# Loads of k and q in quarters, v's rows stored earlier, weight pieces spread over six heads

## The reference

```
h = ln(x) * (1 + scale_msa) + shift_msa
q, k, v = h @ Wq + bq, h @ Wk + bk, h @ Wv + bv      # split into 16 heads of 32
A = softmax(q k^T / sqrt(32));  out = A v
x = x + gate_msa * (out @ Wo + bo)
h2 = ln(x) * (1 + scale_mlp) + shift_mlp
y = x + gate_mlp * (gelu(h2 @ W1 + b1) @ W2 + b2)
```

## Time and profile before

| | us |
|---|---|
| median of 3 runs | 2544.93 (2541.89 to 2549.74) |
| the profiled execution | 2552.45 |
| its span | 2550.7 |
| TensorE busy | 2414.3 (95%) |
| VectorE busy | 1745.4 (68%) |
| ScalarE busy | 1423.4 (56%) |
| GpSimd busy | 1502.3 (59%) |
| DMA, mean over the span | 82 GB/s |

### The profile page before, as it was taken

How to read it: one execution, slowest core, us unless ns; L and a number is a source line. 1 busy time by engine, 2 the same in 40 slices (tenths; PEclk the granted TensorE clock), 3 DMA queues, 4 the chain that set the end, 5 groups by cost and what they waited for, 6 DMA issues and landing times.

```text
span 2550.7 us, 49502 instructions
## 1 busy us (share of the span) xinstructions
PE 2414.3 (95%) x19544; PEld 1358.2 (53%) x19544; DVE 1745.4 (68%) x2878; ACT 1423.4 (56%) x2622; POOL 1502.3 (59%) x706
## 2 busy tenths in 40 slices
PE   6999855899999999999999999999999888999998
PEld 4788642344444444444444444444444346888887
DVE  4444544788888888887888888788878326666563
ACT  3233203577777777777777777777777542222221
POOL 0000103488788878887887888788878634232330
PEclk9999986799999999999999999999999888999999
DMA  7655532122222222222222222222222111332200
GB/s 268 208 171 186 137 110 89 45 75 58 67 72 71 58 68 72 66 62 69 75 57 66 75 69 57 67 77 62 61 71 74 49 50 39 93 103 68 66 34 34
DMA packets 204948, 210.33 MB, mean 82 GB/s; under 512 B 112384, under 2 KB 145152, under 8 KB 195328
## 3 DMA queue, kind: packets, MB, share of 16 engines
q1 hardware_dynamic: 202224, 205.56, 26.9%
q10 hardware_dynamic: 2512, 1.86, 0.3%
HBM read 146.30 MB, written 60.82 MB: 81 GB/s over the span
## 4 chain that ended last, share of the span: by engine, by line
PE 83%; DMA 8%; DVE 3%; ACT 3%; issue 2%; SPq 1%; POOL 0%; ACTq 0%; POOLq 0%; DVEq 0%
PE ps L1216 19%; PE ps L1347 19%; PE ps L1313 9%; PE ps L1325 9%; PE ps L1456 7%; PE ps L1338 7%; PE ps L1327 5%; PE ps L1329 4%; DMA partial_sums<-work 4%; PE ps L1334 2%; DMA q_lo<-work 2%; DVE part_max L1042 1%; ACT work L813 1%; PE ps L1225 1%; DMA tmp<-in_wo 1%
## 5 line engine op out<-in xcount | busy, mean ns | idle before, releaser
L686 POOL TENSOR_TENSOR work<-work 128x1024 f32<-128x1024 f32 x576 | 1351.5, 2405 | 413.9 <-PE ps L1338 223.1
L1042 DVE TENSOR_REDUCE part_max<-ps 128x1 f32<-128x512 f32 x1984 | 1233.2, 682 | 287.7 <-PE ps L1313 287.5
L835 ACT ACTIVATE work<-ps 128x512 f32<-128x512 f32 x2048 | 1058.4, 603 | 355.2 <-PE ps L1334 323.3
L1347 PE MATMUL ps<-work 128*32 128x512 f32 x4096 | 557.7, 617 | 0.2 <-ACT work L835 0.2
L1313 PE MATMUL ps<-acts_r 32*128 32x512 f32 x1344 | 419.2, 480 | 24.7 <-DVE part_max L1042 18.7
L1216 PE MATMUL ps<-acts_r,weights_r 128*128 128x512 f32 x1536 | 383.6, 400 | 4.9 <-DVE acts_r L962 3.8
L1216 PEld LDWEIGHTS ps<-acts_r,weights_r 128*128 128x128 f32 x1536 | 293.5, 193 | 70.2 <-issue 6.8
L1325 PE MATMUL ps<-acts_r 32*128 32x512 f32 x1408 | 300.9, 475 | 28.9 <-DVE work L975 20.0
L1325 PEld LDWEIGHTS ps<-acts_r 32*128 32x128 f32 x1408 | 145.8, 187 | 339.4 <-DVE part_max L1042 176.6
L1327 PE MATMUL ps<-acts_r 32*128 32x512 f32 x1408 | 260.9, 401 | 0.0
L1313 PEld LDWEIGHTS ps<-acts_r 32*128 32x128 f32 x1344 | 181.5, 186 | 140.5 <-DVE part_max L1042 111.4
(11 more groups left out here) (88 smaller groups left out, 2542.9 us busy)
## 6 DMA issues: line engine op xcount, KB each, us to landing
acts_r<-k_hi SPq DMA_DIRECT2D x32, 1024.0 KB
acts_r<-k_lo SPq DMA_DIRECT2D x32, 1024.0 KB
work<-in_x SPq DMA_DIRECT2D x16, 1024.0 KB, 5.4
q_hi<-work SPq DMA_DIRECT2D x32, 256.0 KB, 2.6
q_lo<-work SPq DMA_DIRECT2D x32, 256.0 KB, 3.3
k_hi<-work SPq DMA_DIRECT2D x32, 256.0 KB, 2.6
k_lo<-work SPq DMA_DIRECT2D x32, 256.0 KB, 3.2
v_rows<-work SPq DMA_DIRECT2D x32, 256.0 KB, 2.0
```

What stands on the lines that cost most here:

```text
L686: nc.gpsimd.tensor_tensor(psum_acc[:, at], first, prob[:, t % RING, at], ALU.add).then_inc(add_ok, 1)
L835: nc.scalar.activation(prob[:, t % RING, j * CH:(j + 1) * CH], ps[:, bank, :], ACT.Exp, scale=SCALE).then_inc(exp_ok, 1)
L1042: nc.vector.tensor_reduce(part_max[:, r * TT + q // NQ, q % NQ:q % NQ + 1], ps[:, bank, :], AX.X, ALU.max).then_inc(a_max, 1)
L1347: mm = nc.tensor.matmul(ps[j * DH:(j + 1) * DH, O_BANK, :], v_sb[g % TWO][:, t, :], prob[:, t % RING, j * CH:(j + 1) * CH], start=(t == 0) ...
```

## The change

`load_k` and `load_q` issue four transfers of 32 rows each, one for each row group, instead of one transfer whose outermost dimension is 4; the counts that are waited for (`LOADS_HI`, `LOADS_LO`) follow. In SP's list chunk 7's first four stores come between k_hi and k_lo of head 0, and v's tiles 1 to 3 before head 1's loads. The first two late pieces are loaded before the loads of v of head 1, q_lo and k_lo of head 1 and q_hi and k_hi of head 2; the others two by two at the end of SP's turns for heads 0 to 4. ACT and VectorE split them at steps 4 and 11 of heads 0 to 5. Head 0 makes no maxima in step 0, and has four extra sets, at steps 3, 6, 9 and 12, instead of three.

```diff
-EXTRA_AT = (2, 6, 10)
+EXTRA_AT = (3, 6, 9, 12)
-LOADS_HI, LOADS_LO, LOADS_0 = 2, 3, 6
+LOADS_HI, LOADS_LO, LOADS_0 = 2 * NQ, 2 * NQ + 1, 6
...
-                if g < G - 2 or g == G - 2 and t < NT - LEAD:
+                if (g or t) and g < G - 2 or g == G - 2 and t < NT - LEAD:
...
-        LATE_STEP = 2
+        LATE_STEPS = (4, 11)
+        LATE_HEADS = len(late) // len(LATE_STEPS)
...
             def load_k(dst, src, g, done):
-                rows = src[1][g * DH:(g + 1) * DH, :].rearrange("(o d) q -> o d q", o=1).broadcast_to((NQ, DH, L))
-                sp.dma_start(dst.bitcast(F32), rows).then_inc(done, 16)
+                for r in range(NQ):
+                    sp.dma_start(dst[r * DH:(r + 1) * DH, :].bitcast(F32), src[1][g * DH:(g + 1) * DH, :]).then_inc(done, 16)
 
             def load_q(dst, src, g, done):
-                rows = src[0][g * DH:(g + 1) * DH, :].rearrange("d (r q) -> r d q", q=CH)
-                sp.dma_start(dst.bitcast(F32), rows).then_inc(done, 16)
+                for r in range(NQ):
+                    sp.dma_start(dst[r * DH:(r + 1) * DH, :].bitcast(F32),
+                                 src[0][g * DH:(g + 1) * DH, r * CH:(r + 1) * CH]).then_inc(done, 16)
...
+            def load_late(g):
+
+                for k in range(g * len(LATE_STEPS), (g + 1) * len(LATE_STEPS)):
+                    if k >= 2:
+                        sp.wait_ge(late_hi, k - 1)
+                        sp.wait_ge(late_lo, k - 1)
+                    sp.dma_start(tmp3[:, k % 2, :], late[k][0]).then_inc(late_in[k % 2], 16)
+
             def head(g):
...
                 store_head(g - 1, (g - 1) % TWO)
+                if g + 1 < LATE_HEADS:
+                    load_late(g + 1)
...
             load_k(k_hi[0], qk_hi, 0, hi_in[0])
+            store_qk(NCHUNK - 1, *ORDER[NCHUNK - 1], range(KC))
             load_k(k_lo[0], qk_lo, 0, lo_in[0])
-            store_qk(NCHUNK - 1, *ORDER[NCHUNK - 1])
+            store_qk(NCHUNK - 1, *ORDER[NCHUNK - 1], range(KC, 2 * KC))
             store_v(NCHUNK - 1, *ORDER[NCHUNK - 1], range(1))
             sp.wait_ge(a_max, FILLS)
             load_q(q_hi[0], qk_hi, 0, hi_in[0])
+            store_v(NCHUNK - 1, *ORDER[NCHUNK - 1], range(1, 3))
             put_max(0, 0)
+            store_v(NCHUNK - 1, *ORDER[NCHUNK - 1], range(3, TT))
             load_hi(1, 1)
-            store_v(NCHUNK - 1, *ORDER[NCHUNK - 1], range(1, TT))
-            for k, (rows, _) in enumerate(late):
-                if k == 0:
-                    sp.wait_ge(ada_mm, ADA)
-                if k >= 2:
-                    sp.wait_ge(late_hi, k - 1)
-                    sp.wait_ge(late_lo, k - 1)
-                sp.dma_start(tmp3[:, k % 2, :], rows).then_inc(late_in[k % 2], 16)
-                if k == 1:
-                    sp.wait_ge(qkv_mm, NCHUNK * MM_CHUNK)
-                    stored(NCHUNK)
-                    load_v(1, 1)
-                    load_hi(2, 2)
-                    load_lo(1, 1)
+            sp.wait_ge(ada_mm, ADA)
+            load_late(0)
+            sp.wait_ge(qkv_mm, NCHUNK * MM_CHUNK)
+            load_v(1, 1)
+            load_lo(1, 1)
+            load_hi(2, 2)
+            stored(NCHUNK)
             put_max(1, 1)
+            load_late(1)
...
-            probs(0, {LATE_STEP + k: lambda k=k: split_late_hi(k) for k in range(len(late))})
+            probs(0, late_pieces(0))
...
-            head(0, {LATE_STEP + k: lambda k=k: split_late_lo(k) for k in range(len(late))})
-            for g in range(1, G - 1):
-                head(g)
+            for g in range(G - 1):
+                first = g * len(LATE_STEPS)
+                head(g, {t: lambda k=first + i: split_late_lo(k) for i, t in enumerate(LATE_STEPS) if g < LATE_HEADS})
```

More of the change, by code:

```diff
@@ L840, in probs, with late_pieces @@
                         between[t]()
-            probs(0, {LATE_STEP + k: lambda k=k: split_late_hi(k) for k in range(len(late))})
+            def late_pieces(g):
+                first = g * len(LATE_STEPS)
+                return {t: lambda k=first + i: split_late_hi(k) for i, t in enumerate(LATE_STEPS) if g < LATE_HEADS}
+            probs(0, late_pieces(0))
             for i in range(2):
@@ L845, in _ @@
             for g in range(1, G - 1):
-                probs(g)
+                probs(g, late_pieces(g))
             def split_first_oT(half):
```

## The result

| | before | after |
|---|---|---|
| median of 5 runs, us | 2544.93 (2540.25 to 2549.74) | 2524.05 (2520.45 to 2527.38) |
| the profiled execution | 2552.45 | 2520.45 |
| its span | 2550.7 | 2518.7 |

The change makes the kernel faster by 0.8%: ratio 0.9921, 95% interval 0.9903 to 0.994, which is 20.9 us between the medians. The forecast was 80.6 us, and 2524 us lies outside its range.

A forecast was written before the change was run, and what follows sets the result against it. TensorE was taken to bound the kernel, busy 95% of the span, with stops around head 0's start. Terms -19.7 - 18.8 - 38.1 - 4.0 = -80.6 us took 2544.9 to 2464 us, range 2440 to 2494.

The forecast's parts named there:

- Rival (a): Loads of q and k: quarter transfers no faster than whole ones, rate near 100 GB/s; +25, 2489 us; chance 0.10.
- Parts 1 and 2: Before head 0: chunk 7's stores between split k loads, -19.7 us; v's rows ahead of head 1's loads, -18.8 us.
- The fifth product's margin of 0.3 us: Chunk 7: the fifth product's store lands at about 335 us, wanted by ACT at 335.3.
- Rival (e): Chunk 7 and v's rows: half of the stops stays, 20 us each not won; 2504 us; chance 0.07.
- (b): Head 0: the new waits don't come, clock stays up, extra maxima cost 0.8 us each; 2447 us; chance 0.20.
- Part 3: Head 0: two weight pieces instead of twelve, with new waits and extra maxima; 60.2 against 98.3 us, -38.1 us.
- Part 4: Heads after head 0: faster loads -6 us, ten weight pieces in heads 1 to 5 +2 us; -4 us in all.
- Rival (c): Heads 1 to 5: weight pieces break VectorE's rhythm and the banks, 2.5 us each; +23, 2487 us; chance 0.10.
- The other heads: Heads after head 0: 50.12 us on average against 49.74 at best, 11 us to win; faster loads taken as -6.
- Rival (d): Every head: loads on all engines delay the store of partial sums, stopping ACT and TensorE; 2578 us; chance 0.03.

The follow-up runs named there:

- e5: The kernel before with only the q and k loads in four transfers of 32 rows each; 2503.0 us, ratio 0.9825.
- e6: The kernel of e4 with the q and k loads whole again, as before; 2512.7 us.
- e4: The changed kernel with the weight pieces moved to steps 15, 0 and 1, where GpSimd is idle; 2471.7 us, ratio 0.9706.
- e1: The changed kernel with VectorE's half of each weight piece a maximum with one SBUF input, remainders left out; 2491.6 us.
- e2: The changed kernel with VectorE's half of each weight piece done for one column of 512, both inputs in SBUF; 2516.3 us.
- e3: The changed kernel with VectorE's half of each piece one step after ACT's, at steps 5 and 12; 2510.3 us.
- e8: The changed kernel with GpSimd instead of VectorE making the remainders of the weight pieces, between its additions; 2467.9 us, ratio 0.9689.

## Why the prediction was wrong, point by point

**Four engines against sixteen, right.** From 325 to 330 us after, with k_lo in flight:

```profile
325.00:330.00 5.00, 5.00 (x24) 4.03 (x23) 4.52 (x8) 0.96 (x2) 0.00 (x0) 1.00 1.03 204
```

Share 1.03 at 204 GB/s, where I had taken 200 to 215. e5 and e6 show the cause by doing and undoing that part alone. Rival (a) is out, and with it, for loads of this shape, the rule of the Trainium skill, page DMA: Bandwidth & Descriptors, section Rules for kernel authors, against two transfers to disjoint halves of the partitions instead of one over all 128: the traces don't agree with it for a transfer that stood at a share of 0.25.

**Parts 1 and 2, right.** -38.5 us forecast up to the first score, -40.1 measured after the 2.6 us that came from elsewhere. The fifth product's margin of 0.3 us did not hold: ACT sat idle 4.43 us for its store, 3.04 of them its usual pace, so it was 1.4 us late. TensorE stands nowhere over 0.8 us in these stretches. Rival (e), that half of the stops stays, did not come about; its 2504 counted both stops whole, and half of 18.3 and 20.0 us would have been 19 us, 2483. Nor did (b): head 1's loads did stop TensorE, for 7.3 us.

**Part 3, right in kind, too large by 15.6 us.** Head 1's loads cost 7.3 us, not 4, inside the bound of 8; the waits for the first maxima and exponentials, forecast at 1 and 1.6, were 0.2 and none, so that these three come to 7.5 where 6.6 was forecast. The two pieces were taken as free in head 0 and cost two stops of 2.1 and 2.4 us with a low clock after each. e4 has no piece in head 0's steps 4 and 11 and takes 419.25 - 350.50 = 68.8 us instead of 75.7: so 7 us of the miss are the pieces. Of the other 8 to 9, 1 is the waits; the rest is the clock behind them (0.50 still from 360 to 365 us) and the extra maxima, and how these share it was not taken apart.

**Part 4, the step that failed.** The prediction counted each of the ten pieces in heads 1 to 5 as 0.69 us of VectorE and 0 to 0.8 us of TensorE, "I take 0.2: +2"; they cost 46 to 49 us (+46.3 against before, 297.2 - 5 x 49.74 = 48.5 against a head that runs full), nearly 5 us each. The 48.5 are 31.7 us in which TensorE stands and 17.1 in which it works longer for the same matmuls (265.1 us busy in the five heads against 5 x 49.59 in a head that runs full), at a clock of 0.93 instead of 1.00. Three things were mis-sized in a row:

- The duration. I took 0.69 us from one row. The group of that line over head 0 of before was in the trace, in the view of groups by line (count, busy us, mean ns):

```profile
L1074 DVE TENSOR_TENSOR weights_r<-tmp,weights_r 128x512 fp32r<-128x512 f32 x12 | 14.9, 1242 | 29.6 <-ACT weights_r L795 29.6
```

 A mean of 1242 ns where the least is 691 says that something else holds the operation, and in before's head 0 GpSimd was busy for only 43.0 of 98.3 us, so even this mean was too low for a full head, where it is 2.5 us in the median. e1, e2 and e4 show that it is the second SBUF input beside GpSimd. The Trainium skill has this rule, page SBUF — State Buffer, section Who interferes with whom: a VectorE instruction with two SBUF inputs contends with a GpSimd instruction that reads SBUF, and the second to issue blocks until the first is done. The runs agree with it on who is held, 0.68 us where GpSimd is idle and 2.0 to 4.3 us beside its additions in the change, but not always on how long: in e3 three additions ended during one wait of 7.3 us. I had not weighed the rule.
- The wait for ACT's half, 0.9 us each, stood in no term of the sum. In e1, where the hold is gone, this wait and the 0.69 us of work together cost 2.6 to 3.8 us a head.
- The price of being late. I let VectorE catch up at 0.25 us a step and TensorE lose at most 0.8 us. But VectorE was 2.9 to 5.3 us late at once, more than the banks cover, so TensorE stood for 2.4 to 4.8 us, and behind such stops its clock was lower: heads 1 to 5 run at 0.92 to 0.94. In e1, with stops of at most 1.3 us, it is 0.99 over the five heads.

Rival (c) named the place, VectorE's rhythm and the banks, and gave it 0.10 and 2.5 us a piece, a price from one set of reductions. It did not name the hold by GpSimd, and its 2487 is still 37 us too low. The mean of the group would not have given the price either, but it would have told that 0.69 was the wrong duration.

**The other heads, right.** 49.74 us from head 6 on, all that could be won: heads 6 to 28 gave 8.5 us, and ACT waits for the store of partial sums nowhere from 426 to 1900 us. Rival (d) is out. With the pieces out of VectorE's way the whole comes to 2468 to 2472 us (e8, e4), where 2464 was forecast, so that no other term is far off in sum. That is luck in part. Between the profiled executions of before and after, head 0's other 8 to 9 us are made up for by gains that the forecast had smaller or not at all: 4.2 us up to the first score (2.6 of them outside the change), 3.5 in heads 6 to 28 and 4.6 in the rest, which nothing here explains.

One reading of the start was loose: the clock row says 0.9 or more and not full, and it sinks again, to 8, in slices 32 to 34, where the last stage begins. No term hangs on it.

## What to carry to other kernels

Spreading small work over steps with room is only safe where the engine that does it isn't held by another: compare the least and the mean duration of the same operation in the trace, and put it where the mean is close to the least. A step's free time on one engine is not the margin; what counts is how long the engine behind it can go on with the buffers it has, and for TensorE whether its clock is lower behind the stop (0.99 over the five heads of e1 with stops of at most 1.3 us, 0.93 in the change with stops of 2.4 to 4.8). And when a DMA's share stands at a round fraction of the engines, as 0.25 here, look at its outermost dimension before moving it in the queue.

## What was not expected of the hardware

- A VectorE operation held by GpSimd is not always let in when GpSimd's current operation ends: in e3 it waited 7.3 us for the end of a row of back-to-back additions of 2.3 to 2.4 us, in each of heads 1 to 5. At 445.63 us after the change it got in within 2.47 us, while GpSimd's row went on to 450.31; that row of four took 9.80 us, 0.44 more than the 9.36 of four in head 0 (at 401.52), which fits VectorE's operation having run between two of them. In heads 2 and 4 of the changed kernel itself it waited for the end of the row. What decides between the two was not found out.
- One column held by GpSimd takes 1.47 us in the median, so cutting such an operation down saves little: 8 us of 48 for 511 of 512 columns here.
